# A decoder layer on one core: another hand-written order of all engines and of the DMA queue in the pair loop

## The reference

```python
raw = (xn @ Wq + bq) @ (xn @ Wk + bk).T / 16
# self attention: mean of three softmaxes over raw: causal, over means of 4 keys,
# and over raw with all but the 64 largest of a row set to 0
x = x + mean_of_three(raw) @ V @ Wo + bo
q, k, v = heads(norm(x) @ Wq2.T), heads(ctx @ Wk2.T), heads(ctx @ Wv2.T)
x = x + softmax(q @ k.T + mask) @ v @ Wo2.T          # per head
x = x + dequant(quant(gelu(dequant(quant(norm(x)) @ quant(W1).T))) @ quant(W2).T)
```

## Time and profile before

| | |
|---|---|
| runs (3) | 1853.37, 1856.58, 1858.12 us |
| profiled execution | 1855.2 us, span 1853.4 us |
| busy over the span | PE 85%, PEld 77%, DVE 80%, ACT 56%, POOL 56% |
| TensorE clock granted, mean | 0.977 of full speed |
| 1100 us inside the loop (400 to 1500) | PE busy 984.69, DVE 932.18, POOL 724.69, ACT 629.15 us |

### The profile page before, as it was taken

How to read it: one execution, slowest core, us unless ns; L and a number is a source line. 1 busy time by engine, 2 the same in 40 slices (tenths; PEclk the granted TensorE clock), 3 DMA queues, 4 the chain that set the end, 5 groups by cost and what they waited for, 6 DMA issues and landing times. The chain is left out here.

```text
span 1853.4 us, 50879 instructions
## 1 busy us (share of the span) xinstructions
PE 1581.8 (85%) x15009; PEld 1421.8 (77%) x15028; DVE 1486.3 (80%) x6209; ACT 1043.5 (56%) x2181; POOL 1030.2 (56%) x1156
## 2 busy tenths in 40 slices
PE   5378898888888899888888888888888899848898
PEld 4268888888888888888888888888888888734366
DVE  5567888888888888888888888888888888539886
ACT  2145555555555555555555555555555555429975
POOL 0046666666666666666666666666666666623000
PEclk8699999999999999999999999999999999979999
DMA  5033333333333333333333333333333333332045
GB/s 165 26 82 76 94 93 91 92 90 91 91 90 93 90 90 87 87 86 86 86 86 87 90 93 93 93 93 93 93 93 93 93 93 82 82 103 91 23 161 181
DMA packets 139173, 171.72 MB, mean 93 GB/s; under 512 B 18560, under 2 KB 122240, under 8 KB 139136
## 3 DMA queue, kind: packets, MB, share of 16 engines
q1 hardware_dynamic: 135680, 168.89, 34.3%
q10 hardware_dynamic: 3456, 2.37, 0.5%
HBM read 45.36 MB, written 25.17 MB: 38 GB/s over the span
## 5 line engine op out<-in xcount | busy, mean ns | idle before, releaser
L602 POOL TENSOR_TENSOR shifted<-scores,score_max 128x512 f32<-128x512 f32 x256 | 264.6, 1039 | 298.0 <-DVE score_max L1125 297.0
L608 POOL TENSOR_TENSOR exp_t<-exp_copy,exp_t 128x512 f16<-128x512 f32 x256 | 301.1, 1176 | 132.4 <-ACT exp_copy L962 132.4
L1125 DVE CUSTOM_DVE_ANT_0 scores<-banks,mask 128x128 f32<-128x128 f32 x1024 | 235.8, 286 | 78.3 <-PE banks L796 65.8
L796 PE MATMUL banks<-k_stack,q_stack 128*128 128x128 f16 x2048 | 159.2, 221 | 76.0 <-DMA q_stack<-q_t 49.5
L796 PEld LDWEIGHTS banks<-k_stack,q_stack 128*128 128x128 f16 x2048 | 121.4, 98 | 107.7 <-issue 62.9
L947 ACT ACTIVATE v_nat<-banks 128x512 f16<-128x512 f32 x128 | 77.1, 602 | 211.3 <-PE banks L109 210.1
L107 PE MATMUL banks<-ctx_t,cross_Wk 128*128 128x256 f32 x512 | 153.5, 300 | 26.1 <-DVE ctx_t L1093 25.1
L594 POOL TENSOR_TENSOR k_t<-kv_copy,k_t 128x512 f16<-128x512 f32 x128 | 150.2, 1182 | 30.0 <-ACT kv_copy L950 30.0
L804 PE MATMUL banks<-ident,shifted 128*128 128x128 f32 x1024 | 157.5, 276 | 9.8 <-POOL shifted L602 9.8
L960 ACT ACTIVATE exp_t<-banks 128x512 f16<-128x512 f32 x256 | 154.1, 602 | 15.2 <-PE banks L109 11.2
L962 ACT ACTIVATE exp_copy<-banks 128x512 f32<-128x512 f32 x256 | 156.3, 610 | 0.0
(11 more groups left out here) (245 smaller groups left out, 5723.1 us busy)
## 6 DMA issues: line engine op xcount, KB each, us to landing
k_stack<-k_t SPq DMA_DIRECT2D x256, 256.0 KB, 4.7
q_stack<-q_t SPq DMA_DIRECT2D x512, 64.0 KB, 2.0
x_in<-in_x_dram SPq DMA_DIRECT2D x32, 256.0 KB, 2.7
ctx_in<-in_ctx_dram SPq DMA_DIRECT2D x32, 256.0 KB, 2.8
x_residual<-x SPq DMA_DIRECT2D x64, 128.0 KB, 1.7
x_normalised<-normed SPq DMA_DIRECT2D x32, 256.0 KB, 2.2
shared<-x_normalised SPq DMA_DIRECT2D x8, 1024.0 KB, 5.4
shared<-x_residual SPq DMA_DIRECT2D x16, 512.0 KB, 3.8
```

The source lines that it names most:

```text
L602: pool.tensor_tensor(shifted[:, q % 2], scores[:, q % 2], score_max[:, q % 2, :].unsqueeze(2).to_broadcast([P, QUAD, P]), ALU.subtract).th ...
L608: pool.tensor_tensor(exp_t[:, q % 2, LO], exp_copy[:, q % 2], exp_t[:, q % 2, HI], ALU.subtract).then_inc(exp_split, 1)
L796: mm = pe.matmul(bank[:, tile(h)], q_stack[:, parity, t, tok(b)], k_stack[:, part, parity, t, tok(b)], start=(part == HI), stop=(part == LO))
L1125: op = dve.tensor_tensor_reduce(scores[:, q % 2, h, :], sc_bank(q)[:, tile(h)], mask[:, b, :], 1.0, NEG, ALU.add, ALU.max, score_max[:, q ...
```

## The change

New orders for PE, ACT, DVE, POOL and SP in `body`, and with them a new table of job numbers. The same instructions are issued, with two kinds of exceptions: `fold_value` and `values` now wait themselves for the low half of X and of CTX (in the new order no earlier step does it for them), and ACT's `hi` can wait for late readers of its tile, which for these numbers finds none. The change is described as a new order for which the deviation of the second residual (`x2_deviation`) and the key stack (`stack_keys`) were counted at their real lengths.

```diff
-(J_PT0, J_K0, J_PT1, J_K1, J_AO, J_X, J_K2, J_G, J_V1, J_V0, J_RAW, J_K3, J_X1, J_VV0,
- J_Q0, J_Q1, J_VV1, J_Q2, J_Q3, J_VV2, J_VV3, J_CTX) = range(22)
+(J_K0, J_K1, J_PT0, J_PT1, J_K2, J_AO, J_X, J_K3, J_V0, J_V1, J_G, J_X1, J_RAW, J_VV0,
+ J_Q1, J_Q0, J_Q2, J_VV1, J_Q3, J_VV2, J_VV3, J_CTX) = range(22)
...
                 def fold_value(b, n):
+                    evacuated(J_X, n)
                     bank = begin(J_V0 if b == 0 else J_V1)
...
                 def values(m, n):
+                    evacuated(J_CTX, n)
                     k, b, half = J_VV[m], m // 2, m % 2
...
                 def hi(k, n):
                     act.wait_ge(fj_full, fj(i, k))
+                    late = [u for u in read_by(k) if fj(iteration(-1, u), u) > fj(iteration(0, k), k)]
+                    if late and not first(n):
+
+                        u = max(late, key=lambda u: fj(iteration(-1, u), u))
+                        act.wait_ge(fj_full, fj(iteration(n - 1, u), u))
```

More of the change, by code:

```diff
@@ L636, in body @@
                 if back:
+                    shift(3, i - 1)
+                if front:
+                    lo(J_K0, i)
+                if back:
+                    shift(4, i - 1)
                     exp_lo(1, i - 1)
-                    shift(3, i - 1)
-                    shift(4, i - 1)
-                    exp_lo(2, i - 1)
                 if ahead:
@@ L653, in body @@
                 if back:
-                    exp_lo(4, i - 1)
-                    shift(6, i - 1)
-                    shift(7, i - 1)
+                    exp_lo(3, i - 1)
                 if front:
@@ L863, in body @@
                     x_transpose(i + 1)
+                if front:
+                    keys(3, i)
+                if ahead:
+                    fold_value(0, i + 1)
+                if back:
+                    weigh(1, i - 1)
+                if ahead:
+                    fold_value(1, i + 1)
+                    fold_query(i + 1)
                 if back:
                     weigh(2, i - 1)
[L866 to L870, removed]
                     heads_transpose(0, i - 1)
[L872 to L875, removed]
                     exp_transpose(5, i - 1)
[L877 to L883, removed]
                 if front:
@@ L886, in body @@
                 if back:
+                    weigh(3, i - 1)
+                if ahead:
+                    raw_scores(i + 1)
+                if front:
+                    values(0, i)
+                if back:
+                    exp_transpose(6, i - 1)
                     weigh(4, i - 1)
+                if front:
+                    queries(1, i)
+                if back:
                     heads_transpose(1, i - 1)
                 if front:
-                    values(0, i)
                     queries(0, i)
@@ L997, in body @@
                 if front:
[L998 to L1001 removed]
+                    hi(J_K2, i)
                 if ahead:
@@ L1004, in body @@
                 if front:
-                    hi(J_K2, i)
+                    hi(J_K3, i)
+                if ahead:
+                    hi(J_V0, i + 1)
+                    hi(J_V1, i + 1)
+                if back:
+                    exponential(3, i - 1)
                 if ahead:
@@ L1259, in body @@
                 if back:
+                    add_mask(5, i - 1)
+                if front:
+                    first_residual(i)
+                if ahead:
+                    normalise(i + 1, x_in, moments, rstd, rstd_x, xn, xn_ready)
+                if front:
+                    statistics(i, x1, stats1, stats_x1, moments1, moments_x1)
+                if ahead:
+                    lo(J_X, i + 1)
+                if back:
                     add_mask(6, i - 1)
@@ L1262, in body @@
                 if ahead:
-                    normalise(i + 1, x_in, moments, rstd, rstd_x, xn, xn_ready)
-                if front:
-                    first_residual(i)
-                if ahead:
-                    lo(J_X, i + 1)
+                    lo(J_V0, i + 1)
                 if back:
                     divide(1, i - 1)
+                    add_mask(7, i - 1)
                 if front:
-                    statistics(i, x1, stats1, stats_x1, moments1, moments_x1)
+                    normalise(i, x1, moments1, rstd1, rstd_x1, xn1, xn1_ready)
+                if ahead:
+                    lo(J_V1, i + 1)
                 if back:
```

202 lines of the change are left out of this document (95 added, 107 removed).

## The result

| kernel | runs | median us | range | ratio to before, 95% interval |
|---|---|---|---|---|
| before | 4 | 1855.55 | 1853.37 to 1858.12 | |
| after | 4 | 1881.16 | 1877.88 to 1882.27 | 1.0135 [1.0115, 1.0154] |

The forecast was 1828 us (1790 to 1868). The profiled execution took 1882.18 us, with a span of 1880.4 and a mean granted clock of 0.94 against 0.977.

The account below looks back on a forecast made before the run. The prediction took a ring of hand-overs, its longest link on the DMA queue, as the bound: a walk of 45.9 us plus 1.0 for one lost race, 0.9 less a pass, 27 us over thirty from 1855.2, giving 1828 us (1790 to 1868).

Parts of the forecast that it names:

- the new ring: Chain of hand-overs between engines and DMA queue that sets one loop pass; 45.9 us in the new order against 47.78.
- The slower rival: POOL and DVE exclude each other at all three places; 3.0 us lost, a pass of 48.9 us, 1889 us; chance 0.20.
- The walk: Adding up one pass of the new order with the old durations: 45.9 us, or 46.9 with one race lost.
- all three races won: Rival: DVE loses no time to POOL at three places; 45.9 us a pass, 1799 us; chance 0.25.
- The way to Q0's stack: On SP's queue the key stack ends near 24.3, Q0's stack starts at 26.7, first score at 31.8, 3.2 us sooner.
- Where DVE's chain starts: Statistics of the next x wait for x_in and start 5.2 us into the pass, against 5.65 before; `mix` fits just before.
- a new wait of PE for `probs` at PT0: Sign of a wrong forecast: `mix` at the end of the pass, not x_in, starts DVE's chain.
- Given back: `score(2)` waits for the third query stack, not before 38.9 us; PE stands still about 1.5 us a pass.
- a lost race: DVE held at one place by POOL's running instruction: 0.8 to 1.1 us on DVE's chain; 1.0 us a pass charged.
- The races: Three places where DVE may meet POOL: `normalise` of x against `shift(5)`, of x1 against `exp_lo(3)`, and `mix` against K0's low half.
- One lost of three: The forecast case: DVE held by POOL at one of three places, 1.0 us, a pass of 46.9 us; chance 0.35.
- The written-out passes: Passes outside the hardware loop; the forecast had them gain nothing, against 27 us for thirty passes.

Follow-up runs that it names:

- e1: The changed kernel with 60 one-column memsets on DVE ahead of its loop, shifting the loop in the instruction stream: 1761.47 us, ratio to before 0.9479.
- e4: The changed kernel with 24 transposes of the identity, results unused, on PE ahead of the third key projection in each loop pass: 1841.89 us, ratio to before 0.9918.
- e10: e1 with `mix` put ahead of `largest_of_x2` on DVE, so it starts about 0.7 us earlier: 1747.55 us, ratio to before 0.9422.
- e6: e1 with `mix` moved on DVE from the end of the pass to behind the low half of the context, ahead of `add_mask(3)`: 1823.98 us, ratio to before 0.9832.

## Why the prediction was wrong

The step that failed opens the part on the change: "It removes no work and adds a few waits on PE that are long fulfilled when they are reached", put "at nothing", and from it "So the sum is the length of the new ring". The ring was walked from one first key projection to the next as if the engines ran on without end. But DVE's pass ends in a jump, and its cost was no row of before, because the loop of before happened to lie where it cost nothing. The written-out passes of the new text have 21 more DVE instructions ahead of the loop, and I counted only how instructions move within a pass. In its place the runs show 80 us for the jumps and 39 us for the clock behind them.

No rival had it. The slower rival had POOL and DVE exclude each other at three places, and of these only one was lost. It came to a pass of 48.9 us and 1889, near the 48.9 and 1881 measured, for another reason: that is luck.

The walk itself was also too long. With the jump out of the way e1 took 1761 us, below the range of 1790 to 1868 and below "all three races won" at 1799. A pass took 44.8 us where the forecast had 46.9.

- **The jump back**: 0 forecast; 80 us by e4 and e1. The Trainium skill, page Runtime: NRT & Kernel Launch, section Instruction fetch mechanics, has the mechanism: instructions are held in two blocks of 256 for most engines and fetched ahead in sequence only, and a taken branch whose target is not in the two must fetch first. The packets of the instruction queue and the shifts agree with it; it gives no price, and the runs have 1.7 to 2.8 us a jump; what sets the price at a place was not tested. With the page's blocks of 256, as an estimate, a loop of n instructions touches a third block at n - 257 of 256 starts. For the 294 or 295 of the built program these are 37 or 38 starts, too few for the misses, which span 41 (366 to 406); for the 310 or 311 rows of the trace they are 53 or 54, which has room for all six misses between the fits at 345 and 426. So the blocks of 256 agree with the nine places, but they are inferred; the border itself was not found.
- **The clock**: not in the forecast; 39 us by e4.
- **The way to Q0's stack**: right. In e1 the pass starts at 803.08, and SP's timeline, which answers to the earlier trace rows, reads

```profile
821.49 6.96 SPq L544 DMA_DIRECT2D k_stack<-k_t  x8
830.49 2.38 SPq L534 DMA_DIRECT2D q_stack<-q_t  x4
833.21 0.35 SPq L528 DMA_DIRECT2D mask<-in_fside_Bx1xSxS_dram  x1
833.66 9.33 SPq L534 DMA_DIRECT2D q_stack<-q_t  x12
```

The key stack ends at 25.4 in the pass (24.3 forecast), SP then stands idle, and Q0's stack starts at 27.4 (26.7). PE's first score comes at 32.0 (31.8), without a wait:

```profile
835.08 0.62 PE L807 MATMUL banks<-k_stack,q_stack 128*128 128x128 f16 x8
...
840.52 0.62 PE L807 MATMUL banks<-k_stack,q_stack 128*128 128x128 f16 x8
```

- **Where DVE's chain starts**: the forecast named as a sign of being wrong "a new wait of PE for `probs` at PT0", and it came, two waits a pass, 24.0 us between 400 and 1500 us in e1. There the statistics of the next x start 6.2 us into the pass (5.2 forecast), without a wait, right behind the products of `mix` and three short steps. x_in, issued at 805.61, had landed 2.8 us later, 0.8 us before they start. So in e1 `mix` at its new place, and not x_in, starts the chain, if only by 0.8 us:

```profile
805.61 0.40 SPq L519 DMA_DIRECT2D x_in<-in_x_dram  x1
```
```profile
806.44 2.30 DVE L1224 SCALAR_TENSOR_TENSOR probs<-comp_e,weights,sparse_in 128x128 f32<-128x128 f32 x2
809.25 0.74 DVE L1118 BATCH_NORM_STATS2 stats<-x_in 128x6 f32<-128x256 f32 x2
```

- **Given back**: mis-sized. The second of the two scores above, at 840.52, is `score(2)`, 37.4 into the pass, where I had put "not before 38.9", and PE did not wait for it. I took 12.2 us from the first issue to a usable third stack, 3.98 + 6.28 + 1.90. The first part was 3.17 us, since the first stack took 2.38 instead of 3.18 us to issue. The second was 4.96 (833.66 to 838.62): the third stack is issued from 836.23 on,

```profile
836.23 2.39 SPq L534 DMA_DIRECT2D q_stack<-q_t  x4
```

so the twelve DMAs of 833.66 are not even. My two thirds of 9.42 held in before, where SP stood idle ahead of that stack (first issues at 837.69 and 841.50), and not here. The third part is no more than 1.90, since PE came 1.90 behind the last issue and did not wait. The stack's DMAs landed 2.0 us behind their start in the median; those of before's first stack, right behind the key stack's, took 2.4 to 4.2. Here e1's third stack and then before's first:

```profile
DMA to landing us min/median/max: 1.9/2.0/2.0
DMA to landing us min/median/max: 2.4/3.1/4.2
```

So nothing was given back: the 1.5 us of standing still on PE did not come, nor did the forecast's sign for it, a wait of PE for `q_stack` at `score(1)` and `score(2)`, of which e1 has none between 400 and 1500 us. This is 1.5 us a pass, 45 us of the 67 by which e1 is below my number. The rest is in the main the 1.0 us for a lost race (below).

- **The races**: the two norms were won in the kernel as changed, and so was the first piece of `mix`; its products were lost, once each:

```profile
L1222 DVE SCALAR_TENSOR_TENSOR probs<-comp_e,weights,sparse_in x64: 343/1123/1250, 90.0 to 1598.0; 128x128 f32<-128x128 f32 x64
```
```profile
L1126 DVE TENSOR_SCALAR xn<-x_in,moments,rstd x64: 402/405/815, 60.8 to 1557.8; 128x256 f32<-128x256 f32 x64
```

"One lost of three" was right as a count, at two of POOL's instructions instead of one. The median of the products was 0.34 us before. This is what the Trainium skill's page SBUF — State Buffer, section Who interferes with whom, says of a DVE instruction with two inputs in SBUF, and what I had said no row showed. POOL's rows at that time end where the two products end (814.12 and 815.16; the pair runs 813.02 to 815.31):

```profile
812.95 1.17 POOL L598 TENSOR_TENSOR k_t<-kv_copy,k_t 128x512 f16<-128x512 f32 x1 [1.12 <-ACT kv_copy L963]
814.08 1.08 POOL L606 TENSOR_TENSOR shifted<-scores,score_max 128x512 f32<-128x512 f32 x1
```

- **What a lost race costs**: I charged 1.0 us a pass at its end, on top of a walk whose start of DVE's chain was already 1.0 us too early. In e1 both products were lost, and the pass was still below the 45.9 us of the walk without the charge. One of the two won back gave 0.4 (e10). But a lost race one step further on, ahead of the normalised x, went with 62 us in e6, where PE's wait for it came back at 2.0 us and the clock fell behind it in most passes.
- **The written-out passes**, "nothing": the first interval gained 6.8 us in after and 6.2 in e1. From before to e1 the span falls by 92.1 us, the 29 intervals within the loop by 3.04 each, 88; so about 4 are left for all that is written out, with the 60 memsets in it.
- A slip in the text: K3 was PE's twenty-third step from the first key projection on, not its twenty-fourth. Nothing rests on it.

## What to carry to other kernels

Where an engine's loop is long, as the 310 instructions of DVE here, ask of a change to anything ahead of it or in it whether the jump back still finds its target. Two signs show the miss: a wait put down to issue at the first instruction of the pass, and a count of packets in the instruction queue that grows with the passes. A few dozen idle instructions ahead of the loop test it at no cost that could be measured (90 of them left the old order at 1856 us). Try more than one count and look at the packets, since 60 cured the new order, but 40 did not, and 24 or 60 made the old order 99 and 122 us worse. Before an order is judged, it should be measured at a place that fits. And a stand-still of PE can cost its length and then the clock: here, with one of 2.2 to 3.1 us in each pass of the loop, filling it won 39 us though the stall of DVE stayed whole.

## What was not expected of the hardware

- The jump back of DVE's loop of 294 or 295 instructions in the built program (310 or 311 rows in the trace) shows no wait at some places and 1.7 to 2.8 us at others, with 5 packets a jump on the instruction queue; two places (405 and 406) had a second wait for issue in the pass as well.
- PE's granted clock was 0.50 for the 4.6 us behind a wait of 2.83 us in which PE had almost nothing to do, and 0.57 in the mean of 4 us behind one of 2.19 us (e6); behind another of 2.19 us in e6 it stayed at 1.00. Around the 1.65 us of the earlier trace rows the pass kept 1.00.
- GpSimd's instruction holds a DVE product with two inputs in SBUF to its end: 1.12 instead of 0.34 us.
- 24 superfluous transposes in every pass made the kernel 2% faster (1841.89 against 1881.16 us, e4).
- The four DMAs of the first query stack landed 2.4 to 4.2 us behind their start where the key stack's had just been issued (before), and those of the third stack 2.0 (e1).
